# Reordering the first transfers and splits of a four-layer expert kernel: one output block's weights earlier in SyncE's queue, three experts on VectorE, the first low part of tile 0 on GpSimd

## The reference

```
x = x + L0(x):  w = sum over 8 experts of cond[b,g] * weight[g] * mask;  x @ w.T + bias
x = x + L1(x):  one expert per row (argmax of cond); down(silu(up(x)) * gate(x)), hidden width 512
x = x + L2(x):  the two best experts and a shared one; down(gelu(gate(x)) * up(x)), hidden width 1024
x = x + L3(x):  x @ W_base.T + b_base + 2 * (low-rank update summed over 8 experts with cond)
```

## Time and profile before

| what | us |
|---|---|
| median of 3 runs | 500.3 (500.19 to 500.34) |
| the profiled execution | 499.37 |
| its span on the core | 497.6 |
| TensorE busy | 492.9 (99% of the span) |
| VectorE busy | 343.8 |
| ScalarE busy | 261.6 |
| GpSimd busy | 9.7 |

### The profile page before, as it was taken

One profiled execution on the slowest core, in us unless ns is written; L12 is line 12 of the kernel. 1 busy time (PEld: TensorE's weight loads), 2 busy tenths in 40 slices (PEclk: granted clock), 3 DMA queues, 4 the chain that ended last, 5 costly groups with the idle time before them and its releaser, 6 DMA issues.

```text
span 497.6 us, 6556 instructions
## 1 busy us (share of the span) xinstructions
PE 492.9 (99%) x2175; PEld 406.6 (82%) x2175; DVE 343.8 (69%) x602; ACT 261.6 (53%) x416; POOL 9.7 (2%) x14
## 2 busy tenths in 40 slices
PE   8999999999999999999999999999999999999997
PEld 6788788888888888888888888888888888888886
DVE  4858996877778676866766766566575666655645
ACT  5675463566655353555664445455554555444441
POOL 0510000000000000000000000000000000000000
PEclk9999999999999999999999999999999999999999
DMA  8905332332333343233333333232333232331002
GB/s 326 378 38 169 105 95 90 95 97 96 98 97 100 92 133 97 66 97 95 98 101 101 105 114 95 72 103 81 112 95 110 69 124 95 95 97 32 2 0 84
DMA packets 20480, 51.58 MB, mean 104 GB/s; under 512 B 2784, under 2 KB 3552, under 8 KB 20448
## 3 DMA queue, kind: packets, MB, share of 16 engines
q1 hardware_dynamic: 19872, 50.13, 32.2%
q10 hardware_dynamic: 576, 1.05, 0.6%
HBM read 49.07 MB, written 2.10 MB: 103 GB/s over the span
## 4 chain that ended last, share of the span: by engine, by line
PE 98%; DMA 1%; ACTq 0%; issue 0%; DVE 0%
PE act_ps L292 10%; PE act_ps L293 10%; PE act_ps L294 10%; PE lin_ps L293 10%; PE lin_ps L292 10%; PE lin_ps L294 10%; PE acc_ps L292 10%; PE acc_ps L293 10%; PE acc_ps L294 10%; PE aux_ps L292 1%; DMA cols_w<-w_in 1%; PE aux_ps L294 1%; PE aux_ps L293 1%; PE acc_ps L361 1%; ACTq L234 0%
## 5 line engine op out<-in xcount | busy, mean ns | idle before, releaser
L774 DVE TENSOR_TENSOR hid<-lin_ps,act 128x512 f32<-128x512 f32 x96 | 66.4, 692 | 98.0 <-PE lin_ps L294 97.9
L763 DVE TENSOR_TENSOR w_lo<-raw,w_hi 128x384 fp32r<-128x384 f32 (+1 forms) x221 | 122.9, 557 | 0.0
L491 ACT ACTIVATE hid_hi<-hid 128x512 fp32r<-128x512 f32 x112 | 70.8, 632 | 92.0 <-DVE hid L774 77.2
L485 ACT ACTIVATE act<-act_ps 128x512 f32<-128x512 f32 x96 | 57.3, 597 | 115.0 <-PE act_ps L294 115.0
L782 DVE TENSOR_TENSOR hid_lo<-hid,hid_hi 128x512 fp32r<-128x512 f32 x112 | 77.4, 691 | 26.0 <-ACT hid_hi L491 26.0
L471 ACT ACTIVATE w_hi<-raw 128x768 fp32r<-128x768 f32 x111 | 93.0, 838 | 0.0
L292 PE MATMUL act_ps<-x_hi,w_hi 128*128 128x512 f32 x228 | 88.6, 388 | 0.2 <-issue 0.2
L294 PE MATMUL act_ps<-x_hi,w_lo 128*128 128x512 f32 x228 | 88.5, 388 | 0.0
L293 PE MATMUL act_ps<-x_lo,w_hi 128*128 128x512 f32 x228 | 88.5, 388 | 0.0
L292 PE MATMUL lin_ps<-x_hi,w_hi 128*128 128x512 f32 (+1 forms) x226 | 87.7, 388 | 0.0
L294 PE MATMUL lin_ps<-x_hi,w_lo 128*128 128x512 f32 (+1 forms) x226 | 87.7, 388 | 0.0
(11 more groups left out here) (103 smaller groups left out, 327.1 us busy)
## 6 DMA issues: line engine op xcount, KB each, us to landing
raw<-w_in SPq DMA_DIRECT2D x112, 384.0 KB, 3.1
x<-x_in SPq DMA_DIRECT2D x4, 512.0 KB, 6.4
out<-x SPq DMA_DIRECT2D x7, 256.0 KB, 3.6
cols_w<-w_in ACTq DMA_DIRECT2D x4, 256.0 KB, 5.2
cols_w<-w_in SPq DMA_DIRECT2D x2, 256.0 KB, 5.6
cols_w<-w_in SPq DMA_DIRECT2D x1, 288.0 KB, 3.6
mask<-mask_in SPq DMA_DIRECT2D x1, 256.0 KB, 5.3
cols_w<-w_in SPq DMA_DIRECT2D x2, 128.0 KB, 6.7
```

Source lines behind the costliest of these rows:

```text
L485: act_e.activation(act[:, n % 2, :], act_ps[:, n % 2, :], func, bias=bias).then_inc(act_ready, 1)
L491: act_e.activation(hid_hi[:, n % 2, :], hid[:, n % 2, :], ACT.Copy).then_inc(hid_hi_ready, 1)
L763: ins = dve.tensor_tensor(w_lo[:, n % SPLIT, a:z], raw[:, n % RAW, a:z], w_hi[:, n % SPLIT, a:z].bitcast(F32), ALU.subtract)
L774: ins = dve.tensor_tensor(hid[:, n % 2, :], lin_ps[:, n % 2, :], act[:, n % 2, :], ALU.mult)
```

## The change

The changed kernel moves piece 6 of the weights (block 1, experts 4 and 5) ahead of the mask and `x` in SyncE's queue, and loads row 0 of `x` as two transfers with a semaphore each. TensorE sums five experts of block 0 and VectorE three; in block 1 TensorE takes the experts in the order 0, 1, 4, 5, 2, 3, 6, 7. There is one matmul on zeros less. ScalarE's table load for silu stands ahead of the first split of the summed weights, and tile 0's high parts stand behind those of layer 0's block 1. The low part of tile 0's first 384 columns goes from VectorE to GpSimd, in two instructions of 256 and 128 columns.

```
-PE_EXPERTS = 6
+PE_EXPERTS = 5
...
-WARMUP = 17
+WARMUP = 16
...
             load_w0(sp, 0)
             load_w0(sp, 2)
+            load_w0(sp, 6)
             sp.dma_start(mask[:, :], mask_d).then_inc(mask_in, 16)
-            sp.dma_start(x_row(x_flat, 0), x_d[0]).then_inc(x_in[0], 16)
-            for q in (6, 7, 8):
-                load_w0(sp, q)
+            for c in range(CB):
+                sp.dma_start(x_part(x_flat, 0, c), x_d[0, :, c, :]).then_inc(x0_in[c], 16)
+            load_w0(sp, 7)
+            load_w0(sp, 8)
...
                 if n < 2 and c == 0:
-                    pe.wait_ge(w_lo_c0_ready, n + 1)
+                    pe.wait_ge(w_lo_c0_ready[n], 2 - n)
...
-                experts = PE_EXPERTS if m == 0 else E
-                for g in range(experts):
+                experts = range(PE_EXPERTS) if m == 0 else (0, 1, 4, 5, 2, 3, 6, 7)
+                for g in experts:
...
             def split_x0(b):
-                act_e.wait_ge(x_in[b], 16)
+                if b >= 1:
+                    act_e.wait_ge(x_in[b], 16)
...
                 for c in range(CB):
+                    if b == 0:
+                        act_e.wait_ge(x0_in[c], 16)
...
+            prime(0)
             split_w0(0, 0)
             split_x0(0)
-            prime(0)
+            split_w0(0, 1)
             split_weights0(0)
-            split_w0(0, 1)
-            split_weights0(1)
             split_x1(0)
             split_x1(1)
+            split_weights0(1)
             split_weights(1)
...
             mask_row0(1)
-            split_weights(0, 0)
             split_w0(0, 1)
...
             split_x(1, 0, 1)
+            dve.wait_ge(w_lo_c0_ready[0], 2)
             split_weights(0, 1)
...
+            pool.wait_ge(w_hi_c0_ready, 1)
+            for a, z in ((0, D), (D, D + P)):
+                pool.tensor_tensor(w_lo[:, 0, a:z], raw[:, 0, a:z], w_hi[:, 0, a:z].bitcast(F32),
+                                   ALU.subtract).then_inc(w_lo_c0_ready[0], 1)
             pool.wait_ge(rep_scaled_ready, 1)
```

More of the change, by code:

```diff
@@ L130, in build @@
         aux_ps = psum("aux_ps", [P, CB, T])
+        x0_in = [sem(f"x0_in{c}") for c in range(CB)]
         x_in = [sem(f"x_in{b}") for b in range(B)]
@@ L166, in build @@
         w_lo_ready = sem("w_lo_ready")
-        w_lo_c0_ready = sem("w_lo_c0_ready")
+        w_lo_c0_ready = [sem(f"w_lo_c0_ready{n}") for n in range(2)]
         act_done = sem("act_done")
@@ L361, in sum_row0 @@
                     mm = pe.matmul(acc_ps[:, m, 0:D], diag[:, g, :], w0[:, m, g, :], start=g == 0,
-                                   stop=g == experts - 1)
+                                   stop=g == experts[-1])
                 mm.then_inc(w0_row0_done, 1)
@@ L758, in split_weights @@
                 a, z = part * WT // parts, (part + 1) * WT // parts
[L759 to L762, removed]
+                dve.wait_ge(w_hi_ready, n + 1)
                 ins = dve.tensor_tensor(w_lo[:, n % SPLIT, a:z], raw[:, n % RAW, a:z],
@@ L766, in split_weights @@
                     ins.then_inc(w_lo_ready, 1)
-                elif n < 2:
-                    ins.then_inc(w_lo_c0_ready, 1)
+                elif n == 1:
+                    ins.then_inc(w_lo_c0_ready[1], 1)
             def hidden(n, bias):
```

## The result

| | before | changed |
|---|---|---|
| median, 17 executions each | 499.89 (499.5 to 500.36) | 498.72 (498.44 to 499.33) |
| ratio | | 0.9978, 95% interval 0.9971 to 0.9985 |
| profiled execution, its span | 499.37, 497.6 | 498.45, 496.7 |

The kernel became faster by 0.22%, 1.17 us, with an interval from 0.75 to 1.45 us. The gain forecast was 0.87 us, inside that interval; the time forecast, 499.4 with 498.9 as its lower end, was not met, because before itself had a median of 499.89 over 17 executions and not the 500.3 of its first three.

A forecast was written before the change was run, and what follows sets the result against it. The end of block 1's sum on TensorE was taken to set the end: 0.86 from the sum, 0.05 from VectorE at most, less 0.05, gives 0.87 us, so median 500.3 to 499.4, range 498.9 to 500.0.

The forecast's parts named there:

- What bounds the kernel: Head, first 17 us: the end of block 1's expert sum on TensorE sets the kernel's end; the later stream stays unchanged.
- Piece 6: SyncE's queue: it lands near 6.9 instead of 9.6, the mask at 7.9, the halves of `x` at 8.8 and 9.6.
- The sum: TensorE, block 1: starts at 7.5, no wait left, last pass at 10.74 or 10.84, 0.81 to 0.91 us earlier.
- Three experts: VectorE, block 0: addition at 7.68 instead of 8.06; TensorE's two passes less give 0.43 us of the gain.
- Table load, GpSimd: Head: load and primer covered by ScalarE's wait, next start 8.38; GpSimd's low part hidden, done at 13.6; VectorE gains 0.05 at most.
- the last of the sum: Whole kernel: 0.87 us gain turned into times, span 497.6 to 496.7, median 500.3 to 499.4.
- A larger gain: Transfers in the head: slower flights delay piece 5 and hurt the old chain more; 498.8 to 499.3, chance 0.28.
- TensorE's clock: Expert sum: a later clock rise costs 0.22 more per further pass, nine late passes give 501.3; chance 0.07.
- The late mask: SyncE's transfers: mask landing at 8.8 cuts the gain to 0.5, 499.8; chance 0.13 together with late `x`.
- the worst cases of table load and GpSimd: Head: ScalarE held as long again, gain 0.05, 500.2; or GpSimd ending at 15.0, gain 0.3, 500.0; chance 0.05.

The follow-up runs named there:

- before again: The kernel before, timed once more with nothing changed, for the spread: median 500.27 us, ratio 1.0006 to before.

## Why the prediction was wrong in its time and right in its mechanism

**What bounds the kernel.** Right. Behind 17 us nothing changed (476.84 of 478 us busy against 477.73, with four matmul records fewer, about 0.9 us, which accounts for the difference), and the span followed the stream's first load in 16 of 17 traces; where only the sum came earlier (piece 6 moved alone), it did not move.

**Piece 6.** Landed at 6.97, forecast 6.9. The mask landed at 8.26, forecast 7.9, and cost 0.08 on its chain, inside the slack. The halves of `x` landed at 8.97 and 9.61, forecast 8.8 and 9.6. Piece 7 at 9.96 made a wait of 0.17 where I had none. Block 1's sum began at 7.38 and not at 7.5, as piece 4 came early; the two misses nearly cancel, so that the last pass agrees as well as it does is in part luck.

**The sum.** Last pass 0.90 earlier, forecast 0.81 to 0.91. Mask of block 1 at 11.17 (11.2), first load of the stream at 14.40 (14.44), span 496.7 (496.7).

**Three experts.** Addition at 7.67 (7.68). Its share of the gain was mis-sized: I had 0.43 of the gain from the two passes. The traces of before and changed show 0.30 at block 1's fourth pass, and so 0.60 from the wait that piece 6 fills. Undone, the median loses 0.5.

**Table load, GpSimd.** Covered as forecast (8.33, 13.71). In the traces neither part moved anything: block 1 of layer 0 starts 2.08 behind the sum's last load with them and without. For the low part that is seen only with a last load at 11.17 or later; for an earlier one the spans leave room for anything from 0 to 0.3.

**The step that failed** is the last of the sum: "and the median 500.3, which lies 0.93 above the profiled execution, to 499.4". I took the median of three executions as the level of before and built the range from unknowns of the change alone. The level was 499.89 in 17 executions, of which those three were the first, and between 499.67 and 500.1 on four chips. Of the 0.68 us between the forecast 499.4 and the measured 498.72, 0.41 are this level. From 499.89 the forecast gain gives 499.0, 0.3 above what was measured; the range as I drew it, laid around that, would have held 498.72.

The remaining 0.3 is within the interval of the ratio (a gain of 0.75 to 1.45 us), and its cause is open. The span of the profiled pair gained 0.9 and the medians 1.17, because before's median span lies further above its shortest (0.3 to 0.7 on four chips, with 27 to 35 executions each) than the changed kernel's (0.2 to 0.4, with 12 or 17). For the changed kernel the clock explains spans up to 497.4, as the table of traces shows. For before I estimate that it does not suffice: with the clock up only at 6.9 its first sixteen passes would end some 0.9 later, but 0.6 to 0.7 of that would lie in its wait for piece 5, so its span would grow by about 0.2. Either its clock comes up later than that more often, or piece 5 lands later; without a trace of before at 498.2 or more this can't be told.

**The rivals.** "A larger gain" came nearest in its time. Its mechanism, slow landings that hold piece 5, is neither shown nor refuted: the one other trace of before had piece 5 0.1 later and a span 0.1 longer, and the long executions that were traced, of other kernels, had no late landing. "TensorE's clock" was real, and I had given it 0.07 on the ground that no row put the rise near the edge. One did: the first passes of the earlier trace rows, 16 in 3.85 us where 3.62 would do, are the clock coming up behind the second load of the sum. It didn't decide the result, as none of the 17 executions was long; in the kernels with 16 zeros, five experts and piece 6 moved that were timed later 11 of 58 were, so that was in part luck. Whether the one zero less, which I had costed as neutral, has a share in that tail is not shown: 17 zeros had none in 11. The late mask and the worst cases of table load and GpSimd did not occur.

## What to carry to other kernels

Take the level of before from as many executions as the change is small; with a gain of 0.2% three are too few, and the range must hold the level's spread as well as the change's. When a transfer is moved up in a queue, look at what each engine's program has ahead of the work that it feeds: here the piece alone gained nothing, since a table load and a tile's split stood in front. And count how long TensorE idles between its matmuls on zeros and the first real ones: if the clock may not be up by then, compare the shares of long executions and not only medians.

## What the runs showed that I had not expected

- The time at which TensorE's passes went from 0.43 to 0.216 apart differed from one execution to the next, though the first matmul on zeros starts at 1.04 or 1.05 in every trace: by 5.2 in five traces of 17 (in one of them, before again, at 3.7, among the zeros), between 5.3 and 6.9 in ten, at 9.3 and 9.9 in two. The granted clock is printed as 1.00 in all of these stretches, so here the spacing shows the level and the printed column does not. The Trainium skill ("TensorE: Matmul & The Clock Gate", Part 1) says that the point of transition varies by about 0.5 us either way from run to run. The traces agree that it varies, but by 3.2 us between the first fifteen and by 6 us with the other two.
- With `x` in two transfers on SyncE's queue, piece 5 on ScalarE's queue landed earlier: at 8.5 to 8.8 in the 13 traces with `x` in halves, at 8.8 to 9.3 in the four with `x` whole, with the same bytes on both queues. The nearest pair is the changed kernel (8.7) and the same with `x` in one transfer (9.2). Why, no run shows. In the changed kernel:

```profile
cols_w<-w_in ACTq DMA_DIRECT2D x1, 256.0 KB, 6.5
```

- GpSimd's subtraction of 256 and 128 columns took 0.74 and 0.47 us, 1.17 together, in the changed kernel (1.15 to 1.16 in the other twelve traces that have it), against 0.74 to 1.13 for 256 columns in the earlier trace rows.
